# Graph attention on one core: three of eight weight-word copies of the first supertile given to GpSimd

## The reference, cut to what matters

```python
def L0(h, adj, a):                       # slope 0.01; layer 1 the same with slope 0.2, on h @ W, and elu behind it
    e = (h @ a[:64])[:, None] + (h @ a[64:])[None, :]
    e = where(e > 0, e, slope * e)
    e = where(adj > 0, e, -9e15)
    return softmax(e, axis=1) @ h
x = layernorm(x + L0(x, adj, L0_gnn_a))
x = layernorm(x + L1(x, adj, L1_gnn_W, L1_gnn_a))
```

## Time and profile before

| | |
|---|---|
| median of 3 runs | 456.08 us (455.73 to 457.12) |
| time of the profiled execution | 455.49 us |
| span of its trace, first to last instruction | 453.5 us |
| outside the span | 1.99 us |
| busy in the span | PE 91%, PEld 89%, ACT 85%, DVE 84%, POOL 54% |
| first supertile, masks of step 0 to those of step 7 | about 17.5 to 47.0 us |

### The profile page before, as it was taken

One profiled execution on the slowest core, in us unless ns is written; L12 is line 12 of the kernel. 1 busy time (PEld: TensorE's weight loads), 2 busy tenths in 40 slices (PEclk: granted clock), 3 DMA queues, 4 the chain that ended last, 5 costly groups with the idle time before them and its releaser, 6 DMA issues.

```text
span 453.5 us, 11805 instructions
## 1 busy us (share of the span) xinstructions
PE 413.9 (91%) x4484; PEld 402.7 (89%) x4484; DVE 381.5 (84%) x691; ACT 384.2 (85%) x582; POOL 245.4 (54%) x289
## 2 busy tenths in 40 slices
PE   1699899999999999999978959999999999999980
PEld 1588899999999999999968958999999999999870
DVE  4799897888888798888899957989898988888974
ACT  4897997969799797988798579999999999999830
POOL 6433362755627374481853113749595959595930
PEclk9999999999999999999989988999999999999995
DMA  6999979898998979978000000000000000000000
GB/s 122 101 107 104 88 62 93 71 100 78 85 88 74 99 58 100 86 71 86 3 13 2 11 14 2 1 25 1 25 2 25 0 23 1 23 1 25 1 25 14
DMA packets 22476, 21.66 MB, mean 48 GB/s; under 512 B 1312, under 2 KB 22432, under 8 KB 22432
## 3 DMA queue, kind: packets, MB, share of 16 engines
q0 software_dynamic: 17424, 16.78, 42.5%
q1 hardware_dynamic: 3920, 3.25, 2.2%
q10 hardware_dynamic: 1088, 1.05, 0.7%
HBM read 69.30 MB, written 2.10 MB: 157 GB/s over the span
## 4 chain that ended last, share of the span: by engine, by line
PE 65%; DVE 20%; issue 7%; ACT 5%; POOL 1%; DMA 1%; DVEq 0%; POOLq 0%
PE acc L1154 59%; PE tb L1084 4%; DVE neg L749 4%; DVE pos L760 4%; ACT neg L610 4%; DVE mask_t L678 2%; DVE scr L775 1%; DVE split L735 1%; PE srcb L1094 1%; DMA mask_t<-in_x 1%; DVE odd L671 1%; DVE mask_t L735 1%; ACT wmov L566 1%; DVE mask_t L848 1%; PE pg L1128 1%
## 5 line engine op out<-in xcount | busy, mean ns | idle before, releaser
L1154 PE MATMUL acc<-wmov,pos 128*128 128x195 bf16 x2048 | 368.3, 250 | 15.1 <-DVE pos L760 12.1
L1154 PE MATMUL acc<-wmov,neg 128*128 128x195 bf16 x2048 | 368.3, 251 | 0.0
L610 ACT ACTIVATE neg<-srcb,dcol 128x512 int8<-128x512 f32 x512 | 357.2, 919 | 5.2 <-PE acc L1154 4.9
L1154 PEld LDWEIGHTS acc<-wmov,pos 128*128 128x128 fp8e4 x2048 | 203.3, 99 | 21.5 <-DVE pos L760 17.2
L1154 PEld LDWEIGHTS acc<-wmov,neg 128*128 128x128 fp8e4 x2048 | 202.4, 99 | 2.8 <-issue 1.3
L760 DVE TENSOR_TENSOR pos<-neg,mask_t 128x1024 uint16<-128x1024 uint16 x128 | 105.6, 825 | 18.8 <-PE acc L1154 6.9
L749 DVE TENSOR_TENSOR neg<-neg,mask_t 128x1024 uint16<-128x1024 uint16 x128 | 101.9, 796 | 13.9 <-ACT neg L610 10.1
L444 POOL DMA_DIRECT2D enc<-in_adj x31 | 24.8, 799 | 67.7 <-PE tb L1084 65.8
L678 DVE TENSOR_SCALAR mask_t<-tb 128x512 uint32<-128x512 uint32 (+1 forms) x64 | 43.8, 684 | 13.2 <-PE tb L1084 12.8
L1084 PE MATMUL tb<-ident,enc 128*128 128x128 f32 x256 | 40.3, 282 | 1.5 <-DMA enc<-in_adj 1.4
L671 DVE SCALAR_TENSOR_TENSOR odd<-mask_t,odd 128x1024 uint32<-128x1024 uint32 x32 | 40.5, 1264 | 0.0
(11 more groups left out here) (134 smaller groups left out, 280.2 us busy)
## 6 DMA issues: line engine op xcount, KB each, us to landing
enc<-in_adj POOLq DMA_DIRECT2D x31, 512.0 KB, 8.4
mask_t<-in_x ACTq DMA_DIRECT2D x4, 256.0 KB, 5.1
x_rows<-xout SPq DMA_DIRECT2D x8, 128.0 KB, 3.8
resid<-x_rows SPq DMA_DIRECT2D x8, 128.0 KB, 2.1
out<-xout SPq DMA_DIRECT2D x8, 128.0 KB, 1.7
enc<-in_adj POOLq DMA_DIRECT2D x2, 256.0 KB, 7.9
resid<-in_a SPq DMA_DIRECT2D x1, 64.0 KB, 4.0
resid<-in_w SPq DMA_DIRECT2D x2, 16.0 KB, 4.0
```

Of the source, the lines that this page charges most:

```text
L610: ins = nc.scalar.activation(neg[:, k % SR, :, b], srcb[:, q % 2, :], ACT.Sign, bias=dcol[:, layer, c:c + 1])
L1154: ins = nc.tensor.matmul(acc[t][:, side * WC:(side + 1) * WC], m[:, t * P:(t + 1) * P, b], wmov[:, c, side * WC:(side + 1) * WC], start=fi ...
```

## The change

In the first supertile of layer 0 the copies of groups 1, 3 and 5 (`KEPT`) are made by POOL with a `tensor_copy`, and ACT leaves them out. POOL makes the copy of group g behind the product of group g+1. The copy waits for the first instruction of `weigh` of its group, and raises a new semaphore `w_pool`. Whoever waited for `w_act` (PE ahead of the steps of a first supertile, and `multiply`) now waits for both counts. Sizes, data and results are as before.

```diff
+KEPT = (1, 3, 5)
...
+        w_pool = sem("w_pool")
...
+        def wait_for_copies(eng, n):
+
+            by_pool = sum(g < n for g in KEPT)
+            if by_pool:
+                eng.wait_ge(w_pool, by_pool)
+            eng.wait_ge(w_act, n - by_pool)
...
             if n > 1:
                 eng.wait_ge(w_vec, WEIGH * (n - 1))
-                eng.wait_ge(w_act, n - 1)
+                wait_for_copies(eng, n - 1)
...
             for g in range(KB):
                 multiply(pool, nc.gpsimd, 0, g)
+                if g - 1 in KEPT:
+
+                    w = wmov[:, NB * (g - 1):NB * g].rearrange("p b (s c) -> p b s c", s=2)[:, :, :, 0:2 * FD]
+                    pool.wait_ge(w_vec, WEIGH * (g - 1) + 1)
+                    nc.gpsimd.tensor_copy(w, top_of(0, g - 1).rearrange("p b s r c -> p b s (r c)")).then_inc(w_pool, 1)
...
                         if k == 0:
                             exps_of_d(0, 0, KB * NB, 0)
-                        else:
+                        elif k - 1 not in KEPT:
                             keep_parts(0, k - 1)
...
                     pe.wait_ge(w_vec, WEIGH * (NQ * layer + k + 1))
-                    pe.wait_ge(w_act, NQ * layer + k + 1)
+                    wait_for_copies(pe, NQ * layer + k + 1)
```

## The result

The changed kernel takes 457.79 us (median of 12 runs, 457.06 to 458.84) and the kernel before, run beside it, 455.75 us (12 runs, 454.92 to 457.12). The ratio is 1.0044 with a 95% interval of 1.0032 to 1.0056: slower by 2.04 us, where 1.85 us was forecast. ACT is relieved as intended, and the change costs more than it gives.

What follows compares the result with a forecast made beforehand. DVE was taken to hold the first supertile, PE alone 59 to 210 us. Copies +2.47 us, less 0.62 given back, make +1.85: 457.34 us profiled, median 457.93 (0.59 added), range 456.3 to 459.8 us.

Steps and rivals of the forecast that it cites:

- ACT's relief worth 0: ACT, first supertile: dropping three copies of about 1.07 us, some 3 us of its queue, gains 0 on the path.
- the 2.27 us ahead of copy 7: ACT's idle time before copying group 7, waiting for DVE's L735; read as reserve of its queue, expected to grow.
- Length of the copy: Each POOL copy of 1040 elements in the first supertile was put near 1.07 us.
- The estimate of 1.56 us: Length of a POOL copy by the Trainium skill's 1.8 cycles per element at 1.2 GHz; delay some 3.5 us.
- the slow case: Rival: POOL's copy takes 2.16 us at the product's rate per element; +5.3 us, 461.4 us, tail +7.5 us; chance 0.14.
- Price at DVE: POOL's three copies delay the end of DVE's L749 in steps 1, 3 and 5, by 2.47 us together.
- Copy 5: POOL's copy of group 5: L749 ends at 39.73 instead of 39.06 us, +0.67, two small DVE instructions covering part.
- Given back: Product 6 on POOL no longer waits for an adjacency load, as DVE's masks come later; 0.62 us of delay disappears.
- copy 1: POOL's copy of group 1, behind product 2: DVE's L749 ends at 23.26 instead of 22.32 us, +0.94.
- the cheap case: Rival: POOL copies two bf16 words at a time or frees the port early; about +0.2 us, 456.3 us; chance 0.17.
- an early release as in L344: POOL's one-input L344 gave way before finishing; if copies do likewise, DVE end to DVE end is hardly above 0.80 us.
- The relief of ACT: Rival: ACT held the turn to the second supertile, so DVE's 1.17 us wait shrinks; down to 454.9 us; chance 0.03.

## Why the prediction was right, point by point

- **What bounds the kernel.** Right. DVE holds the first supertile (the 0.58 us that it waits for POOL's product of group 1, ahead of 19.34 us, are its only idle time there), the delay passes through ACT's copy 7 and the signs to PE, and from there it reaches DVE's last instruction whole. The prediction wrote that PE alone sets the pace from 59 to 210 us; what follows it, where DVE and ACT hold the chain in part, it left out, and nothing was absorbed there.
- **ACT's relief worth 0.** Right, shown by leaving the copies out (1.0004, and an entry that moves only with the load). The reason given was wrong in part. The prediction took the 2.27 us ahead of copy 7 for the reserve of ACT's queue and expected them to grow; they stayed 2.27 us. ACT's slack ends at L571 in step 5, where it waits for DVE, and the 2.27 us are only what its work from there on leaves.
- **Length of the copy.** I put it near 1.07 us from the fill and the product; it is 1.06 us. The estimate of 1.56 us that the prediction sets beside it was too long, and the slow case, at the product's rate per element, of 2.16 us, twice too long.
- **Price at DVE.** Forecast 0.94 + 0.86 + 0.67 = 2.47 us. Measured in the full change, by the ends of L763 and with the 0.03 us taken off by which everything started later: 1.00 + 0.84 + 0.80 = 2.64 us. Copy 5 was the term that was mis-sized. I had let two small DVE instructions cover part of it; they are held as well, the first took 1.03 us, and the second and L763 came only after it. From the end of L752 to the end of L763, 1.67 us passed instead of the 1.54 that I took.
- **The step that failed although its number held.** I expected L749 (now L763) to be drawn out to 1.6, 1.5 and 1.3 us, and wrote that the prediction would be wrong if it kept 0.69 us. It kept 0.68 us everywhere. The wait is there, but on whichever instruction came first: L752 in step 1, L739 in step 3, L721 in step 5. In step 1 I had also taken it that the waiting L752 would run before the copy, as the two engines took turns in the earlier trace rows. It did not: POOL's copy started 0.06 us before the product ended and kept the port. The sum is nearly the same, as DVE loses the same reading time either way. The sign to look for was the end of the group of instructions, not the length of one.
- **Given back.** 0.62 us forecast, 0.64 us in the trace. Only in part a property of the kernel: the three profiles of before agree on the moment it ends in, other executions had 0 or 0.8 us of it. The medians do not confirm it: the copies cost 2.04 us with the load where it was and 2.25 us with it moved, and moving the load alone changed nothing (0.9997), with an uncertainty of 0.5 us or more on each. So the median is forecast well by a sum whose term of -0.62 us is seen in traces alone; some of that agreement may be luck.
- **Size.** 1.85 us forecast, 2.07 us at PE's entry, 2.04 us in the median; the masks of step 3 came 1.88 us later (1.8 forecast), those of step 7 2.03 us (1.85 forecast). Of the 0.22 us between forecast and entry, 0.13 are copy 5 and 0.06 copy 1; 0.03 are the later start, and the rest is small differences. The forecast of 457.93 us for the time itself came within 0.14 us of the median, and that is partly luck: it stood on 456.08 us for the kernel before, whose median is 455.75 us beside the new kernel.
- **Range and chances.** The slow copy fell with the row of 1.06 us, and with it the half of the cheap case in which POOL moves two words at a time. The other half, an early release as in L344, fell with the 1.53 us from the end of L752 to the end of L763 in step 3, against 0.80 us. (A one-input instruction that gives the port up early does exist, as the run with `tensor_scalar` shows; the copy is not one.) The relief of ACT fell with its own run.

## What to carry to other kernels

Before work is moved to GpSimd, look at what VectorE is doing at that moment: if it holds the chain and its instructions read two operands of SBUF, expect each microsecond that GpSimd reads to be a microsecond lost, as it nearly was here (2.64 us for three copies of 1.06 us), however idle GpSimd was (54% busy here) and however full the relieved engine (85%). Price such a move by the operand elements that GpSimd reads, not by how long its instruction lasts (0.85 us at DVE for an instruction of 3.21 us here), but look at what else then comes late. And ask what the relieved engine is waited for: ACT idled 2.27 us ahead of the place where the chain passed through it, so relief was worth nothing. An idle time at one place is no measure of the slack of all the work ahead of it, though: look for the last point at which the engine waits for the one that holds the chain.

## What the runs showed of the hardware that I had not expected

- The port is given back when POOL has read, not when it is done: a `tensor_scalar` of 3.21 us held DVE for 0.85 us, a copy of 1.06 us for 0.80 to 1.00 us, that is nearly to its end, a fill of 0.98 us not at all.
- A DVE copy of 4 numbers from SBUF to SBUF (0.16 us) takes 1.02 us beside a POOL copy and 0.41 us beside a POOL fill; a `tensor_scalar` of 8 numbers 1.03 us beside a POOL copy. One-input instructions are held as well, here in float32, and beside the fill they end with it (30.08 against 30.06 us), though what stands behind them is not held.
- Two POOL instructions in a row can keep the port between them though DVE has been waiting since the start of the first: with the copy behind the product DVE waited for both (2.64 us), with the `tensor_scalar` in its place it was let in between (1.65 us). In the rows the copy starts 0.06 us before the product ends and the `tensor_scalar` 0.09 us behind it; whether that decides stays open.
